# A new plan of a row's stages, with a state ring of twelve steps and three units for x

## The chip, the cores and the metric

The kernel runs on one core of one Trainium2 chip. What counts is the time of one execution on the device in microseconds; the kernel before takes 4036.85 us, the median of three runs. Engines are named as in the profile: PE (TensorE), ACT (ScalarE), DVE (VectorE), POOL (GpSimd), and SP, the engine whose queue issues the DMAs here.

## What is computed

The input is x of 8 images, 48x48 tokens, 256 channels. Cut to what matters, the reference is:

```python
x1 = layernorm(x)                                # over 256 channels
xh, z = split(x1 @ W_in)                         # 512 channels each
xc = depthwise_conv3x3(xh)
dt_r, Bp, Cp = split(xc @ W_xproj)               # 8, 16, 16 columns
dt  = softplus(dt_r @ W_dt + b_dt)
dtN = dt @ W_dtN + b_dtN                         # 16 columns
for t in range(48 * 48):                         # one token of each image a step
    h = exp(dt[t] * A) * h + (dtN[t] * Bp[t]) * xc[t]    # h: 8 images x 512 x 16
    y[t] = h @ Cp[t] + Dskip * xc[t]
x = x + (layernorm(y) * ln_g + ln_b) * silu(z) @ W_out + b_out
t = layernorm(x)
x = x + t + ffn(t)     # ffn: thresholds channels, decodes two nibbles and a shift, and adds 2 at one-hot places
```

## The kernel before, in words

The scan over 2304 steps is the backbone. The states lie on 128 partitions (16 states over two halves of channels, for 8 images); each step has 256 columns for each of two states per partition. DVE updates 192 of the 256 columns, POOL the other 64. For a step DVE does four instructions: `decay_state` multiplies the decay in PSUM (ps_a) with the last state (L869, L872), and `add_input` adds db times x and writes the state (L885, L888). ACT makes the decays by Exp: `decay` (L638) for a pair of steps into one of two ps_a buffers, and `decay_pool` (L648) for POOL's part of four steps, a quad. POOL does one `up` (L1149) for a quad and two instructions for a step (L1159, L1169). PE sums the states of a quad into ps_y (`sum_states`, L492), with the skip term in front of every sixteen steps (`add_skip`, L476); ACT copies ps_y out (`copy_y`). The states stay in a ring of `HRING` steps, and a place is used again once its quad is summed (`c_done`). dt and x reach the scan over DRAM: `store_x` and `store_dt` write a row of 48 steps, `load_x` and `load_dt` spread four steps over the partitions (xb with `XUNITS` units, dtb with three), 512 KB each.

A row has 48 steps, called s. Everything else of the kernel is cut into stages which are hung into these steps, by hand, in the program of each engine. In the row i of the scan PE runs the stages of other rows: LayerNorm transposes and the input projection of row i+4, conv, x_project, dt_project, dtn_project and the transposes for row i+1, z of row i, and the output part of row i-1. `SLOT` gives for each PE stage its steps; the ACT instruction that empties the bank follows in the next step (`s - 1 in SLOT[...]`), and `middle` and `after` say what DVE does between its decay and its add, and behind it. All these PE stages share two PSUM banks in turn: a stage may take its bank when the stage two before it in the order has been emptied (`take_bank`, `emptied_before`). Each engine runs its own list in order, so a wait holds all that stands behind it. ACT's `decay` of a pair waits for the state two pairs back, so ACT can be at most about two steps ahead of DVE.

In the plan before, out_project has the steps 29 to 31 and add_residual 30 to 32; conv 0, 1, 3, 4; the FFN of row i-1 (`ffn_stage`, fourteen stages, two in a step) 40 to 46; gate_y on POOL 21 to 24.

## Time and profile before

| | |
|---|---|
| time, median of three runs | 4036.85 us (4023.55 to 4038.51) |
| the profiled execution, its own time | 4022.24 us |
| its span, first to last instruction | 4020.4 us |
| mean granted TensorE clock | 0.854 |
| PE busy | 3251.8 us, 81% |
| DVE busy | 3622.2 us, 90% |
| ACT busy | 2944.1 us, 73% |
| POOL busy | 3133.2 us, 78% |
| DMA moved | 790.26 MB, mean 197 GB/s |

Busy is the time in which an engine has an instruction in work; a matmul's end is modelled, and neighbouring instructions of one engine overlap a little, so that the distance from start to start is the better price of an instruction than its duration. The granted clock is 1.0 for 2.4 GHz and 0.5 for 1.2 GHz. Times in the rows are microseconds from the span's start unless they are marked ns.

### The profile page before, as it was taken

How to read it: one execution, taken by the hardware profiler on the slowest of the kernel's cores; microseconds unless marked ns; L12 is line 12 of the kernel's file. 1: busy time of each engine (PE TensorE's matmuls, PEld its weight loads, DVE VectorE, ACT ScalarE, POOL GpSimd, SP SyncE). 2: the span in 40 equal slices, each digit the busy share in tenths (PEclk: the TensorE clock that was granted, in tenths of full speed). 3: DMA queues.
4: the chain of work that ended last, by engine and by line, in shares of the span. 5: the costliest groups of instructions: out<-in, count | busy, mean ns of one | idle time of the engine just before them, and what ended most of it. 6: DMA issues, size and time to landing. Idle time of an engine off the chain costs nothing.

```text
span 4020.4 us, 103342 instructions
## 1 busy us (share of the span) xinstructions
PE 3251.8 (81%) x33792; PEld 1589.3 (40%) x33792; DVE 3622.2 (90%) x12317; ACT 2944.1 (73%) x6050; POOL 3133.2 (78%) x5771
## 2 busy tenths in 40 slices
PE   5788888888888888888888888888888888888665
PEld 2334433443344334433443344344433343444333
DVE  2799999999999999999999999999999999999996
ACT  3677777777777787777777777777777777787663
POOL 0788877888888788877888788778877888788874
PEclk7889887889889988988898889888888798889776
DMA  3877878788878787878787878787877888788773
GB/s 67 219 202 203 213 191 206 190 208 205 208 196 214 199 211 196 215 194 205 197 216 199 207 196 213 199 205 193 206 201 199 201 203 209 202 206 205 192 192 80
DMA packets 383392, 790.26 MB, mean 197 GB/s; under 512 B 80517, under 2 KB 235142, under 8 KB 382854
## 3 DMA queue, kind: packets, MB, share of 16 engines
q1 hardware_dynamic: 382854, 783.66, 77.1%
q8 instruction: 268, 4.39, 0.5%
q14 instruction: 270, 2.21, 0.2%
HBM read 648.18 MB, written 96.73 MB: 185 GB/s over the span
## 4 chain that ended last, share of the span: by engine, by line
DVE 31%; PE 31%; ACT 26%; issue 7%; SPq 3%; POOL 2%; DMA 1%; ACTq 0%; POOLq 0%; DVEq 0%
ACT ps_a L638 8%; PE ps_s L583 6%; DVE h L885 6%; PE ps_y L492 6%; PE ps_s L528 4%; DVE ps_a L869 4%; DVE ps_a L872 4%; DVE h L888 4%; PE ps_s L537 3%; ACT ap L648 3%; PE ps_s L566 3%; PE ps_y L476 2%; ACT y L721 2%; DVE sz L941 2%; PE ps_s L584 2%
## 5 line engine op out<-in xcount | busy, mean ns | idle before, releaser
L638 ACT ACTIVATE ps_a<-dtb,a_n 128x384 f32<-128x384 f32 x2304 | 1253.6, 583 | 488.1 <-DVE h L888 472.3
L1169 POOL TENSOR_TENSOR h<-mp,up 128x128 f32<-128x128 f32 x2304 | 1052.5, 457 | 357.6 <-PE ps_y L492 147.4
L1159 POOL TENSOR_TENSOR mp<-ap,h 128x128 f32<-128x128 f32 x2304 | 1051.9, 457 | 358.1 <-ACT ap L648 242.7
L869 DVE TENSOR_TENSOR ps_a<-ps_a,h 128x192 f32<-128x192 f32 x2304 | 813.6, 353 | 239.6 <-ACT ps_a L638 236.7
L885 DVE SCALAR_TENSOR_TENSOR h<-xb,db,ps_a 128x192 f32<-128x192 f32 x2304 | 921.9, 400 | 24.0 <-PE ps_y L492 16.0
L888 DVE SCALAR_TENSOR_TENSOR h<-xb,db,ps_a 128x192 f32<-128x192 f32 x2304 | 927.2, 402 | 0.0
L492 PE MATMUL ps_y<-h,cw 64*32 64x256 f32 x18432 | 787.9, 461 | 71.9 <-DVE h L888 58.0
L872 DVE TENSOR_TENSOR ps_a<-ps_a,h 128x192 f32<-128x192 f32 x2304 | 807.7, 351 | 0.0
L648 ACT ACTIVATE ap<-dtb,a_n 128x256 f32<-128x256 f32 x1152 | 524.2, 509 | 251.1 <-DMA dtb<-xd 233.9
L1149 POOL TENSOR_TENSOR up<-xb,db 128x512 f32<-128x512 f32 x576 | 610.8, 1060 | 3.0 <-DMA xb<-xd 3.0
L492 PEld LDWEIGHTS ps_y<-h,cw 64*32 64x32 f32 x18432 | 315.7, 122 | 488.2 <-DVE h L888 244.6
L511 PE MATMUL ps_s<-xlnT,win 128*128 128x384 f32 x768 | 317.4, 552 | 163.4 <-ACT xh L755 127.1
L528 PE MATMUL ps_s<-xs,conv_w 96*32 96x384 f32 x4608 | 409.9, 506 | 16.7 <-ACT xc L656 8.3
L518 PE MATMUL ps_s<-xlnT,win 128*128 128x384 f32 x768 | 288.2, 509 | 27.1 <-DVE sz L941 26.9
L575 PE MATMUL ps_s<-swap,y 128*128 128x128 f32 x576 | 140.5, 391 | 200.5 <-ACT y L721 173.7
L583 PE MATMUL ps_s<-wout,yn 128*128 128x256 f32 x1152 | 295.8, 401 | 5.5 <-POOL yn L1194 5.5
L551 PE MATMUL ps_s<-xp,wdt 9*128 9x384 f32 x384 | 276.4, 850 | 1.0 <-ACT xp L665 1.0
L511 PEld LDWEIGHTS ps_s<-xlnT,win 128*128 128x128 f32 x768 | 146.6, 206 | 295.2 <-ACT xh L755 154.8
L1189 POOL TENSOR_TENSOR dt<-dt,dttok 128x768 f32<-128x768 f32 x96 | 173.7, 1810 | 108.9 <-ACT dt L698 108.9
L528 PEld LDWEIGHTS ps_s<-xs,conv_w 96*32 96x32 f32 x4608 | 148.4, 114 | 262.1 <-issue 252.0
L583 PEld LDWEIGHTS ps_s<-wout,yn 128*128 128x128 f32 x1152 | 212.4, 194 | 83.0 <-issue 43.1
L476 PE MATMUL ps_y<-skip_w,xc 128*32 128x128 f32 x4608 | 178.6, 303 | 45.6 <-ACT y L762 45.6
(111 smaller groups left out, 4286.5 us busy)
## 6 DMA issues: line engine op xcount, KB each, us to landing
xb<-xd SPq DMA_DIRECT2D x576, 512.0 KB, 7.2
dtb<-xd SPq DMA_DIRECT2D x576, 512.0 KB, 6.3
xs<-xh SPq DMA_DIRECT2D x196, 192.0 KB, 6.2
xd<-dttok SPq DMA_DIRECT2D x288, 128.0 KB, 5.4
xin<-in_x_dram SPq DMA_DIRECT2D x144, 128.0 KB, 6.2
xd<-xtok SPq DMA_DIRECT2D x192, 96.0 KB
res<-in_x_dram SPq DMA_DIRECT2D x144, 128.0 KB, 5.4
out_dram<-res SPq DMA_DIRECT2D x144, 128.0 KB, 3.9
```

The source lines that it names most:

```text
L492: mm = pe.matmul(ps_y[32 * j:32 * j + 32, half, 0:HALF], weights[part, q * P + 32 * j:q * P + 32 * j + 32], h[part, (4 * Q + j) % HRING, n ...
L528: mm = pe.matmul(bank[32 * c:32 * c + 32, 0:TOK], conv_w[0:96, r % 3, dx, NG * c + g, :], xs[0:96, g, c, dx * IMAGES:dx * IMAGES + TOK], s ...
L583: pe.matmul(bank[:, 0:DM], yn[:, g, k * P:(k + 1) * P], wout[:, g, :], start=g == 0, stop=False)
L638: ins = act.activation(ps_a[buf][:, n, 0:2 * VD].rearrange("p (t d) -> p t d", t=2), dtb[:, u % DUNITS, 2 * buf:2 * buf + 2, 0:VD], ACT.Ex ...
L648: ins = act.activation(ap[:, Q % 2, :, n, :], dtb[:, Q % DUNITS, :, VD:HALF], ACT.Exp, scale=a_n[:, n:n + 1])
L869: dve.tensor_tensor(a[:, 0], a[:, 0], last[:, 0], ALU.mult).then_inc(m0_done, 1)
L872: dve.tensor_tensor(a[:, 1], a[:, 1], last[:, 1], ALU.mult).then_inc(m1_done, 1)
L885: dve.scalar_tensor_tensor(h[:, G % HRING, 0, 0:VD], x_t, db[:, r % 2, 0, w:w + 1], a[:, 0], ALU.mult, ALU.add).then_inc(h0_ready, 1)
L888: dve.scalar_tensor_tensor(h[:, G % HRING, 1, 0:VD], x_t, db[:, r % 2, 1, w:w + 1], a[:, 1], ALU.mult, ALU.add).then_inc(h_ready, 1)
L1149: pool.tensor_tensor(up[:, Q % 2], x4, db4.broadcast_to([P, 4, 2, VP]), ALU.mult).then_inc(u_ready, 1)
L1159: pool.tensor_tensor(mp[:, G % 2], ap[:, Q % 2, G % 4], h[:, (G - 1) % HRING, :, VD:HALF], ALU.mult) \
L1169: pool.tensor_tensor(h[:, G % HRING, :, VD:HALF], mp[:, G % 2], up[:, Q % 2, G % 4], ALU.add) \
```

## The change

All stages get new steps. Out_project goes to 23, 24, 25 with add_residual in 24, 25, 26; z to 27 to 30; dtn_project to 31 and the transposes of dt to 32, 33, 35; conv to 40 to 43, for row i+2 now; the projection to 0, 2, 10, 11, for row i+3; x_project to 1; dt_project to 3 and 21, in pairs; the transposes of y to 16 to 19. gate_y moves to POOL's steps 18 to 21, finish_dt to 13 and 26. SP's stores of x and dt are cut into three pieces each, and bounce_states and load_states stand in 34 and 37. The FFN of row i-2 runs in steps 0 to 13, one stage in a step, with twelve stages instead of fourteen: the comparison with 0.5 is folded into the instructions that use it. x_project, dt_project and dtn_project are cut into two halves of the tokens that use different parts of the PE array, and xp and dbt hold 24 positions on twice the partitions. The ring of states has twelve steps, and xb three units.

```diff
-B_ROW, C_ROW, XP_ROWS = 32, 64, 80
+B_ROW, C_ROW, XP_ROWS = 32, 48, 64
-HRING = 8
-XUNITS, DUNITS = 4, 3
+HRING = 12
+XUNITS, DUNITS = 3, 3
 SLOT = {
-    "conv": (0, 1, 3, 4), "xproj": (6,), "dtp": (8, 9, 11, 12), "xtok": (14, 15, 16), "yt": (18, 19, 20, 21),
-    "dttok": (23, 24, 26), "dtn": (27,), "out": (29, 30, 31), "z": (33, 34, 36, 37), "xlnT": (39, 40),
-    "proj": (42, 43, 45, 46),
+    "proj": (0, 2, 10, 11), "xproj": (1,), "dtp": (3, 3, 21, 21), "xtok": (6, 7, 9), "yt": (16, 17, 18, 19),
+    "out": (23, 24, 25), "z": (27, 28, 29, 30), "dtn": (31,), "dttok": (32, 33, 35), "conv": (40, 41, 42, 43),
+    "xlnT": (45, 46),
 }
-AHEAD = {"conv": 1, "xproj": 1, "xtok": 1, "dtp": 1, "dttok": 1, "dtn": 1, "xlnT": 4, "proj": 4, "z": 0, "yt": -1, "out": -1}
+AHEAD = {"conv": 2, "xproj": 1, "xtok": 1, "dtp": 1, "dttok": 1, "dtn": 1, "xlnT": 4, "proj": 3, "z": 0, "yt": -1, "out": -1}
...
# SP
-                    if s == 6 and exists(i - 2):
+                    if s in (8, 10, 12) and exists(i + 1):
+                        store_x(i + 1, (8, 10, 12).index(s))
+                    if s == 13 and 0 <= i + 3 <= SIDE:
+                        load_stack(i + 3)
+                    if s == 14 and exists(i - 2):
                         store(i - 2)
-                    if s == 8 and 0 <= i + 3 <= SIDE:
-                        load_stack(i + 3)
-                    if s == 18 and exists(i - 1):
+                    if s == 19 and exists(i - 1):
                         load_residual(i - 1)
-                    if s == 21 and exists(i + 1):
-                        store_x(i + 1)
-                    if s == 26 and exists(i + 1):
-                        store_dt(i + 1)
-                    if s == 30 and exists(i + 1):
+                    if s == 34 and exists(i + 1):
                         bounce_states(i + 1)
-                    if s == 34 and exists(i + 1):
+                    if s in (35, 36, 38) and exists(i + 1):
+                        store_dt(i + 1, (35, 36, 38).index(s))
+                    if s == 37 and exists(i + 1):
                         load_states(i + 1)
-                    if s == 42 and exists(i + 5):
+                    if s == 47 and exists(i + 5):
                         load_xin(i + 5)
...
# PE: x_project; dtn_project likewise
                 for g in range(NG):
-                    mm = pe.matmul(bank[0:XP_ROWS, 0:TOK], wxp[:, g, :], by_step(xc[:, r % 2, g, :]),
-                                   start=g == 0, stop=g == NG - 1)
+                    for half in range(2):
+                        lo = half * XP_ROWS
+                        mm = pe.matmul(bank[lo:lo + XP_ROWS, 0:HTOK], wxp[:, g, :],
+                                       by_step(xc[:, r % 2, g, :])[:, half * QUADS // 2:(half + 1) * QUADS // 2],
+                                       start=g == 0, stop=g == NG - 1, skip_group_check=True)
...
# DVE, and the same on POOL
-                    if u >= 2:
-                        dve.wait_ge(c_done, u - 1)
+                    if u >= HRING // 4:
+                        dve.wait_ge(c_done, u - HRING // 4 + 1)
...
# DVE: ffn_stage
-                    ins = dve.tensor_scalar(hot[:], hot[:], 0.5, None, ALU.is_gt)
+                    for w in range(3):
+                        ins = dve.scalar_tensor_tensor(score[:, :, w, :], hot[:, :, 32 + 8 * w:48 + 8 * w], 0.5,
+                                                       score16[:].unsqueeze(1).broadcast_to([P, KT, 16]),
+                                                       ALU.is_gt, ALU.mult)
...
# DVE: middle
+                if exists(i - 2):
+                    if s < FFN:
+                        ffn_stage(i - 2, s)
+                    if s == 12:
+                        ffn_mark(i - 2)
+                    if s == 13:
+                        ffn_add_low(i - 2)
                 if exists(i - 1):
                     if s == 6:
                         y_stats(i * KT - 1)
-                    if s == 10:
+                    if s == 11:
                         y_shift_by(i - 1)
-                    if s in (30, 31, 32):
-                        add_residual(i - 1, s - 30)
-                    if s in (33, 34, 35):
-                        ln2_stats(i - 1, s - 33)
-                    if 40 <= s < 47:
-                        ffn_stage(i - 1, 2 * (s - 40))
...
+                    if s in (24, 25, 26):
+                        add_residual(i - 1, s - 24)
+                    if s in (26, 27, 28):
+                        ln2_stats(i - 1, s - 26)
...
# POOL
-                    if s in (16, 17) and exists(i + 1):
-                        finish_dt(i + 1, s - 16)
+                    if s in (13, 26) and exists(i + 1):
+                        finish_dt(i + 1, (13, 26).index(s))
...
-                    if s in (21, 22, 23, 24) and exists(i - 1):
-                        gate_y(i - 1, s - 21)
+                    if s in (18, 19, 20, 21) and exists(i - 1):
+                        gate_y(i - 1, s - 18)
```

## Rows read from the trace of the kernel before

**Rows 1.** Page, part 4: shares of the chain by engine.
```profile
DVE 31%; PE 31%; ACT 26%; issue 7%; SPq 3%; POOL 2%; DMA 1%; ACTq 0%; POOLq 0%; DVEq 0%
```

**Rows 2.** Windows view of the whole scan: length, busy us (instructions), clock, DMA share, GB/s.
```profile
117.00:3982.80 3865.80, 3172.37 (x33438) 1547.63 (x33438) 3587.01 (x12202) 2902.35 (x5966) 3122.69 (x5751) 0.86 0.80 202
```

**Rows 3.** Windows view (PE, PEld, DVE, ACT, POOL) of steps 10-18, 28-32, 40-47 of one row.
```profile
2057.68:2073.98 16.30, 11.26 (x118) 5.50 (x116) 12.41 (x46) 16.30 (x35) 13.86 (x24) 0.63 1.01 223
...
2085.94:2095.38 9.44, 9.44 (x66) 6.08 (x65) 7.68 (x25) 4.58 (x9) 8.49 (x18) 1.00 0.94 253
...
2107.28:2123.91 16.63, 13.27 (x130) 5.62 (x133) 16.63 (x62) 8.03 (x17) 11.96 (x25) 0.90 0.76 196
```

**Rows 4.** Waits view, DVE and ACT: us in total, times, longest us.
```profile
DVE ps_a L869 <- ACT ps_a L638: 236.7, 220, 17.7
...
ACT ap L648 <- DMA dtb<-xd: 233.9, 97, 5.0
```

**Rows 5.** Timeline of DVE, last instruction of two bare steps: start us, us, operation.
```profile
117.34 0.41 DVE L888 SCALAR_TENSOR_TENSOR h<-xb,db,ps_a 128x192 f32<-128x192 f32 x1
...
118.52 0.40 DVE L888 SCALAR_TENSOR_TENSOR h<-xb,db,ps_a 128x192 f32<-128x192 f32 x1
```

**Rows 6.** Lines view, small FFN operations of DVE: count, busy us, mean ns, idle before.
```profile
L978 DVE TENSOR_SCALAR hot<-hot 128x192 f32<-128x192 f32 x48 | 40.5, 843 | 0.0
...
L1027 DVE TENSOR_TENSOR res<-res,hots 128x48 f32<-128x48 f32 x48 | 36.8, 768 | 0.1
L992 DVE TENSOR_TENSOR nib<-best,found 128x9 int32<-128x9 f32 x48 | 33.9, 706 | 0.0
...
L1031 DVE TENSOR_TENSOR res<-res,hots 128x48 f32<-128x48 f32 x48 | 9.5, 198 | 0.1
```

**Rows 7.** Timeline of PE, a state sum and two out blocks.
```profile
2084.48 1.09 PE L492 MATMUL ps_y<-h,cw 64*32 64x256 f32 x32
2085.50 1.99 PE L583 MATMUL ps_s<-wout,yn 128*128 128x256 f32 x8
...
2088.05 1.99 PE L583 MATMUL ps_s<-wout,yn 128*128 128x256 f32 x8
```

**Rows 8.** Around conv: windows of one row, PE's timeline in it and the next.
```profile
1956.54:1962.50 5.96, 5.96 (x60) 2.05 (x64) 5.96 (x27) 3.73 (x8) 3.33 (x8) 0.50 0.67 179
1962.50:1968.50 6.00, 6.00 (x92) 2.11 (x88) 6.00 (x21) 4.25 (x9) 2.75 (x6) 0.98 0.67 171
...
1958.43 8.15 PE L528 MATMUL ps_s<-xs,conv_w 96*32 96x384 f32 x72
...
2115.88 2.46 PE L511 MATMUL ps_s<-xlnT,win 128*128 128x384 f32 x4 [3.36 <-ACT xh L755]
...
2120.01 6.01 PE L528 MATMUL ps_s<-xs,conv_w 96*32 96x384 f32 x72
```

**Rows 9.** POOL: timeline of gate, up and two steps; then finish_dt by line.
```profile
2001.97 1.00 POOL L1194 TENSOR_TENSOR yn<-yn,sz 128x384 f32<-128x384 f32 x1
2002.93 1.06 POOL L1149 TENSOR_TENSOR up<-xb,db 128x512 f32<-128x512 f32 x1
...
2007.02 0.46 POOL L1159 TENSOR_TENSOR mp<-ap,h 128x128 f32<-128x128 f32 x1
...
2008.08 0.46 POOL L1159 TENSOR_TENSOR mp<-ap,h 128x128 f32<-128x128 f32 x1
...
L1189 POOL TENSOR_TENSOR dt<-dt,dttok 128x768 f32<-128x768 f32 x96 | 173.7, 1810 | 108.9 <-ACT dt L698 108.9
```

**Rows 10.** Timeline of ACT, a pair of ps_a and what follows it.
```profile
2079.48 1.13 ACT L638 ACTIVATE ps_a<-dtb,a_n 128x384 f32<-128x384 f32 x2
2080.49 1.11 ACT L677 ACTIVATE dttok<-ps_s 128x512 f32<-128x512 f32 x2
```

**Rows 11.** SP's timeline, twelve x stores; then dtb's issues, KB, us to landing.
```profile
1997.46 8.52 SPq L354 DMA_DIRECT2D xd<-xtok  x12
...
dtb<-xd SPq DMA_DIRECT2D x576, 512.0 KB, 6.3
```

More of the change, by code:

```diff
@@ L148, in build @@
         best = sb("best", [P, KT, 3])
-        found = sb("found", [P, KT, 3])
         nib = sb("nib", [P, KT, 3], I32)
@@ L545, in transpose_xc, with dt_project @@
                 mm.then_inc(xtok_done, 1)
-            def dt_project(r, g):
-                if g == 0:
+            def dt_project(r, pair):
+                if pair == 0:
                     pe.wait_ge(xp_ready, r + 1)
-                bank = take_bank("dtp", r, g)
-                pe.matmul(bank[:, 0:TOK], wdt[:, g * P:(g + 1) * P], xp[0:DTR + 1].rearrange("p b w -> p w b"),
-                          start=True, stop=True).then_inc(dtp_done, 1)
+                banks = [take_bank("dtp", r, 2 * pair + half) for half in range(2)]
+                for n in range(2):
+                    g = 2 * pair + n
+                    for half in range(2):
+                        rows = slice(half * XP_ROWS, half * XP_ROWS + DTR + 1)
+                        mm = pe.matmul(banks[half][:, n * HTOK:(n + 1) * HTOK], wdt[rows, g * P:(g + 1) * P],
+                                       xp[rows].rearrange("p b w -> p w b"), start=n == 0, stop=n == 1,
+                                       skip_group_check=True)
+                        if n == 1:
+                            mm.then_inc(dtp_done, 1)
             def transpose_dt(r, k):
@@ L565, in dtn_project @@
                 for g in range(NG):
-                    mm = pe.matmul(bank[0:B_ROW + NS, 0:TOK], wdtn[:, g, :], dt[:, g, :],
-                                   start=g == 0, stop=g == NG - 1)
+                    for half in range(2):
+                        lo = half * XP_ROWS
+                        mm = pe.matmul(bank[lo:lo + XP_ROWS, 0:HTOK], wdtn[:, g, :],
+                                       dt[:, g, half * HTOK:(half + 1) * HTOK],
+                                       start=g == 0, stop=g == NG - 1, skip_group_check=True)
                 mm.then_inc(dtn_done, 1)
@@ L983, in ffn_stage @@
                     ins = dve.tensor_tensor(amp[:], hot[:, :, 39], hot[:, :, 40], ALU.max)
                 elif n == 3:
-                    dve.scalar_tensor_tensor(amp[:], amp[:], 2.0, hot[:, :, 0], ALU.mult, ALU.mult)
-                    ins = dve.tensor_reduce(best[:], score[:], AX_X, ALU.max)
+                    dve.tensor_scalar(nib[:], best[:], -1.0, 16.0, ALU.mult, ALU.add)
+                    ins = dve.tensor_scalar(amp[:], amp[:], 0.5, 2.0, ALU.is_gt, ALU.mult)
                 elif n == 4:
-                    ins = dve.tensor_scalar(found[:], best[:], 0.0, None, ALU.is_gt)
+                    dve.tensor_single_scalar(nib[:], nib[:], 15, ALU.bitwise_and)
@@ L989, in ffn_stage @@
+                    ins = dve.scalar_tensor_tensor(amp[:], hot[:, :, 0], 0.5, amp[:], ALU.is_gt, ALU.mult)
                 elif n == 5:
[L990 removed]
+                    ins = dve.scalar_tensor_tensor(val[:], nib[:, :, 1], 16.0, nib[:, :, 0], ALU.mult, ALU.add)
                 elif n == 6:
[L992 to L995 removed]
@@ L1134, in _ @@
                     after(i, s)
+            for n in range(FFN):
+                ffn_stage(SIDE - 1, n)
+            ffn_mark(SIDE - 1)
+            ffn_weigh(SIDE - 1)
             ffn_add_low(SIDE - 1)
```

229 lines of the change are left out of this document (110 added, 119 removed).

## The prediction

> **What bounds the kernel now.** I read the windows over the scan first, then the chain, then DVE's waits, and last the timelines of single engines inside one image row. From its first to its last state update the scan takes 3865.8 us, and DVE works in 3587.0 of them [rows 2]. The reader is to see that no other engine comes near: POOL 3122.7, ACT 2902.4. Yet DVE has only 31% of the chain; PE has 31% and ACT 26% [rows 1]. So DVE is the bound on the average and hands over in places. The windows of one row of 79.9 us show where: in its steps 10 to 18 DVE works 12.41 of 16.30 us while ACT is busy in all 16.30, and in steps 28 to 32 it works 7.68 of 9.44; in steps 40 to 47, where the FFN stages lie, it works all the time [rows 3]. DVE's waits say the same: 236.7 us for ACT's ps_a, and ACT in turn 233.9 us for dtb [rows 4].
>
> Per row of 48 steps that is 3865.8 / 48 = 80.5 us, of which DVE works 74.7 and stands 5.8. I call the end of DVE's step s T(s).
>
> **What falls away.** (a) The ACT burst of steps 10 to 18: softplus, xtok, y_norm and scale_yn lie there together. The new plan spreads them from step 4 to 25. I estimate ACT's steps 13 to 22: five pairs of ps_a at 1.01, or 5.1 us [rows 10], and fifteen single ACTIVATEs (ap, y_norm, scale_yn, ln1, parts, copy_y) at about half a pair each, 7.6: 12.7 us, against 13.6 of DVE (ten bare steps of 1.18 [rows 5] and 1.8 for ln1 and the last adds). So this stall goes, 3.9 us in the row shown [rows 3]. (b) The stall of steps 28 to 32, 1.8 us in that row, ends with the late dtb load behind twelve x stores in one piece, 8.5 us on SP [rows 11], which are now three pieces. All 5.8 go, and what is late next is worked out below.
> (c) DVE's own work: is_gt on 192 elements goes, 0.84 us a row, and the chain of found, best, nib with its 0.71 us is two short operations; mark and weigh lose one instruction each; make_db works on half the elements a partition [rows 6]. Against it stand three operations with is_gt folded in, one on amp and one bitwise_and. Means of such small operations hold waits: ffn_add_low and ffn_add_high have the same shape and take 0.77 and 0.20 us [rows 6], and a wait can come back at another instruction. Two instructions fewer at 0.2 give 0.4 us a row as the lower bound, is_gt, nib and three more at 0.2 give 2.2 as the upper; I take 1.2.
> The Trainium skill, "SBUF — State Buffer", section "Who interferes with whom", says that a DVE instruction with two SBUF inputs contends with a GpSimd one that reads SBUF, and that the later one blocks in full. By that rule the 0.71 us of nib are a wait for POOL, which may return wherever POOL is busy, and the saving would be near 0.4, not 1.2; the pair of 0.77 and 0.20 agrees with it.
> (d) x_project, dtn_project and dt_project in two halves save PE time, at most half of their matmuls, and the copy of xp half of ACT's. PE has slack there in the new plan (steps 1, 3 and 21 carry one stage each), so I cost this gain at nothing; if the halves don't overlap, it costs nothing either, as long as PE is idle before step 23.
> (e) The ring of twelve lets DVE and POOL go one quad further before they wait for sum_states. DVE hardly waited for that, and I take zero; without it the conv stage below would cost more. With three x units each load has four steps less: it is issued eight steps, 9.4 us, before its use. I take 0, bounds 0 and 1 us a row.
>
> **What comes: the out-projection.** A bare step takes DVE 1.18 us [rows 5]. From T(19) to the first add_residual, in step 24, DVE has four steps, the aggregates, y_stats and the decay half of step 24: 4.7 + 0.3 + 0.6 + 0.6 = 6.2 us. Without a wait the third, in step 26, stands 9.5 us after T(19). PE can't start out 0 before two things. Its bank is that of the third dtp group, which ACT empties in its step 22; ACT's pair of step 22 waits for T(19), then ln1's logarithm, 1.01 for ps_a and as much for the two parts of the same size [rows 10]: T(19) + 2.7. And it needs all four gates of POOL, now in POOL's steps 18 to 21. POOL's step is 1.06 us (start to start of mp), up adds 1.01, a gate 0.96, a finish_dt 1.8 [rows 9]. From T(12) on: I estimate that POOL starts step 12 about 5 us before T(12), four steps of DVE, since it waits only for ap, which ACT makes in step 11; ten steps from 12 to 21, three up, one finish_dt and four gates are 10.6 + 3.0 + 1.8 + 3.8 = 19.3 us, so the last gate ends at T(12) + 14.4, and T(19) is at T(12) + 9.8. Out 0 starts at T(19) + 4.7.
> Now PE: an out block is 2.55 us and sum_states 1.02 [rows 7], the skip of step 24 about the same. Out 0, skip, sum, out 1, out 2 are 9.7 us: T(19) + 14.4 against 9.5, a stall of 4.9 us at full clock. If POOL were in time it would be 2.7.
> The clock: ahead of the old conv PE stands (3.36 us in one row), and conv's stretch begins at 1.2 GHz: granted clock 0.50 in the 6 us where it starts and 0.98 in the next 6. Three groups took 8.15 us there and 6.01 in the other row, where the level had risen by 2120.0, some 4 us after the gap [rows 8]. In the old steps 10 to 18, light on PE, it is 0.63; in steps 28 to 32, where the old out blocks lie behind dttok and dtn, 1.00 [rows 3]. The new plan puts only transposes, sums and one dtp pair ahead of out, so it starts at the half level. With half speed for 4 to 6 us, as in those two rows, the loss is 2 to 3. The whole stall is then 6.9 to 7.9; I take 7.0, bounds 2.7 and 7.9.
> The Trainium skill, "TensorE: Matmul & The Clock Gate", section "Part 1: The HAM clock gate", says that the throttled state is the default and that activity releases it. By it moving matmuls apart costs speed, which speaks against this plan; with a clock that never fell the stall would be 4.9.
>
> **What comes: conv.** It moves from steps 0 to 4, where DVE had FFN work, to steps 40 to 43, where DVE has bare steps. PE's step 40 begins with add_skip, which waits for copy_y of ACT's step 38, so for T(35) + 1.6. Skip, sum and three conv groups of 2.0 [rows 8] end 8.2 us later at full clock, T(35) + 9.8. ACT copies group 2 in step 43 and makes the ps_a pair 44 behind it, 1.5 us more: T(35) + 11.3. DVE wants it at T(43), eight steps and one y_stats on, T(35) + 10.05. So 1.2 us at full clock, and with 2 to 3 lost at the half level (the same gap lies in front of it) 3.2 to 4.2. I take 3.5, bounds 1.2 and 4.2.
> z and dtn: four z banks pass through DVE's make_sz in steps 29 to 32, right behind the late out blocks, with two table loads on ACT: 0.5 us, bounds 0 and 1.
>
> **The sum.** New stalls 7.0 + 3.5 + 0.5 = 11.0 us a row, old ones 5.8, DVE's work 1.2 less: +4.0 us. Over 47 row periods +190; with head and tail unchanged (117.0 us before the first update, 37.6 behind the last [rows 2]; the same stages in new slots) I add 10 for the FFN stages that now run alone behind the last row. The profiled execution took 4022.2 us, so 4222; the median of the three runs lies 14.6 above it, which gives 4237, and I write **4240**. Its own range is 4130 to 4350.
>
> **The rivals.**
> A, the forecast, 0.55.
> B, DVE alone is the bound, 0.20. The last out block would have to be there by T(19) + 9.5 and conv's third group by T(35) + 8.5: POOL ahead by two more steps, PE at full clock. For it: DVE has the largest sum of work [rows 2]; all other engines have 10 us a row to spare. Against it: the order of the queues, and PE's level in light stretches [rows 3, 8]. Price: stalls of 2.3 instead of 5.8, and 1.2 less work, -4.7 us a row: 4037 - 220 = about 3820.
> C, a chain of transfers at the row's end comes on top, 0.15. dttok is now made in steps 32 to 35. SP queues bounce_states (34), store_dt (35, 36), the loads of step 36, load_states (37, which waits for the bounce) and store_dt (38) before the next row's first load_dt in step 40, and that waits for the last store. By SP's 0.7 us an issue and 6.3 for a transfer to land, the median of dtb, taken for the store too [rows 11], dtb is there at T(35) + 14 to 17; ACT needs it in step 47. Up to about T(35) + 16 conv's stall hides it. The same on the other side: store_x, load_stack and store are 19 transfers in SP's steps 8 to 14, and load_residual of step 19 waits for the store to land. If each bounce takes as long as the old one did under load, 4 us a row come: 4430.
> D, B and A cancel, within 0.5% (about what a measurement of this kernel can tell from no change), 0.05: about 4037.
> E, the halves don't run side by side and PE carries 4 us more of old work, 0.05: out starts no later, since PE stands before it; 4250.
>
> **How the numbers follow.** Slower by over 0.5%: A, C and E, 0.75. Within: 0.05. Faster: 0.20. The range must leave out no more than 2 in 10: most of B lies below 3980 (0.13), and the upper part of C above 4390 (0.06). It is 3980 to 4390.
>
> **What the profile after would show.** Right, if add_residual waits for PE's out block in nearly every row, several us in all; the windows of steps 23 to 26 show a granted clock near 0.5 at first; POOL's last gate ends after T(22); DVE's wait for ps_a lies around steps 42 to 45; ACT is no longer busy without a gap in steps 10 to 18. Wrong, if DVE's busy share rises above 95%; if out blocks end before step 24 begins; if the largest wait of ACT is dtb at the row's end (C); if DVE's work falls by more than 2.2 us a row.

## The result and the profile after

The changed kernel takes 4241.88 us, the median of four runs (4239.21 to 4246.69), beside 4030.2 us for the kernel before on the same chip. The ratio is 1.0526, with an interval of 1.0497 to 1.0555. The prediction said 4240. The profiled execution took 4239.21 us, 217 us more than that of the kernel before.

The rows of after are read in the order of the prediction. First the page's part 4, the chain, which answers to [rows 1]:

```profile
DVE 32%; PE 28%; POOL 16%; ACT 10%; issue 9%; SPq 2%; DMA 2%; POOLq 0%; DVEq 0%; ACTq 0%
```

ACT had 26% and has 10; POOL had 2% and has 16; PE had 31% and has 28. The hand-over has moved from ACT's burst to POOL, and PE keeps its part.

The windows view, with length, busy us of PE, PEld, DVE, ACT, POOL, the clock, the DMA share and GB/s. The first row is the scan [rows 2], with some 7 us ahead of its first state update at 124.05; then come steps 10 to 18 of one row [rows 3], steps 24 to 26, and steps 42 to 47:

```profile
117.00:4200.00 4083.00, 3110.67 (x34542) 1669.14 (x34549) 3535.44 (x12039) 2929.90 (x5969) 3130.79 (x5752) 0.82 0.74 191
2091.49:2105.40 13.91, 6.83 (x110) 3.31 (x109) 13.91 (x47) 12.27 (x24) 12.79 (x22) 0.77 0.81 196
...
2112.43:2125.49 13.06, 13.06 (x93) 7.50 (x92) 5.46 (x18) 6.99 (x12) 11.35 (x21) 0.73 0.87 208
...
2148.31:2159.08 10.77, 10.37 (x154) 4.63 (x146) 7.26 (x25) 8.82 (x19) 7.47 (x15) 1.00 0.68 187
```

In steps 10 to 18 DVE now works all 13.91 us, where it worked 12.41 of 16.30. In steps 24 to 26 it works 5.46 of 13.06 while PE is busy throughout, and in steps 42 to 47 it works 7.26 of 10.77. These are the two stalls that the prediction named.

The waits view of DVE and ACT (total us, times, longest us), which answers to [rows 4]:

```profile
DVE ps_a L891 <- ACT ps_a L655: 328.4, 244, 17.5
DVE res L970 <- PE ps_s L602: 238.3, 110, 11.9
```

```profile
ACT ap L665 <- DMA dtb<-xd: 110.5, 89, 3.4
```

The add_residual of line 970 waits 238.3 us in all for PE's out blocks; in the kernel before the same view has 34.8 us for it. ACT waits for dtb half as long as before.

From the trace of each kernel I also took, for rows 2 to 45, the mean distance from one step's state update to the next and DVE's idle time in it. "Work" is the rest. For one row, in us:

| | row | work | idle | where DVE stands |
|---|---|---|---|---|
| before | 80.71 | 75.16 | 5.56 | steps 10, 16, 18: 3.6; 28, 32: 1.8 |
| after | 85.38 | 74.13 | 11.26 | 24 to 26: 6.46; 32, 34: 1.31; 42, 44: 3.44 |

Of the 6.46 us, 4.8 are waits of the three adds for PE and 1.7 are a wait of DVE's step 24 for ACT's ps_a. PE's timeline around out shows where most of it comes from; each line has start, duration, instruction and, in brackets, the idle time before it with its releaser:

```profile
2106.11 2.20 PE L563 MATMUL ps_s<-xp,wdt 9*128 9x192 f32 x8 [0.23 <-ACT yn L790]
2109.93 3.78 PE L601 MATMUL ps_s<-wout,yn 128*128 128x256 f32 x8 [1.62 <-POOL yn L1212]
2113.64 1.22 PE L602 MATMUL ps_s<-bout,ones_row 1*128 1x256 f32 x2
2114.78 1.94 PE L480 MATMUL ps_y<-skip_w,xc 128*32 128x128 f32 x32
2116.65 1.96 PE L496 MATMUL ps_y<-h,cw 64*32 64x256 f32 x32
2118.54 2.45 PE L601 MATMUL ps_s<-wout,yn 128*128 128x256 f32 x8
2120.92 0.69 PE L602 MATMUL ps_s<-bout,ones_row 1*128 1x256 f32 x2
2121.54 1.99 PE L601 MATMUL ps_s<-wout,yn 128*128 128x256 f32 x8
```

Out block 0 waits for POOL's last gate, then takes 3.78 us where out 2, behind it, takes 1.99 [rows 7]. Skip and sum take 1.94 and 1.96, a sum at the full clock 1.09. So PE starts out at 1.2 GHz and rises near 2119. The windows view has a granted clock of 0.50 for this stretch:

```profile
2109.93:2116.00 6.07, 6.07 (x34) 4.15 (x38) 4.28 (x14) 5.11 (x10) 4.46 (x9) 0.50 1.02 244
```

DVE's timeline has the other side of it:

```profile
2113.53 0.37 DVE L891 TENSOR_TENSOR ps_a<-ps_a,h 128x192 f32<-128x192 f32 x1 [0.99 <-ACT ps_a L655]
...
2114.96 0.42 DVE L970 TENSOR_TENSOR res<-res,ps_s 128x256 f32<-128x256 f32 x1 [0.80 <-PE ps_s L602]
...
2121.65 0.42 DVE L970 TENSOR_TENSOR res<-res,ps_s 128x256 f32<-128x256 f32 x1 [4.87 <-PE ps_s L602]
...
2124.20 0.42 DVE L970 TENSOR_TENSOR res<-res,ps_s 128x256 f32<-128x256 f32 x1 [0.94 <-PE ps_s L602]
```

The second add waits 4.87 us, since skip and sum stand between out 0 and out 1. The wait for ACT in front of the first add lies inside the same delay: the third add can't start before out 2 is done, and that sets the sum of the three stalls. Over rows 2 to 45 the last gate ends at T(19) + 2.90, out 0 starts at T(19) + 2.96, and out 2 is done 12.98 us later: T(19) + 15.9 beside the 9.5 at which the third add stands without a wait.

### The profile page after: what moved, and what is told of

Read it like the earlier page. It is cut to its first block, busy times and chain, and to the rows that moved or that the text cites. A ratio compares the mean times of both kernels' runs of the same rounds, so it can differ in the third digit from the quotient of the medians.

```text
span 4237.4 us, 105655 instructions
## 1 busy us (share of the span) xinstructions
PE 3185.6 (75%) x34944; PEld 1709.0 (40%) x34944; DVE 3571.5 (84%) x12174; ACT 2969.7 (70%) x6050; POOL 3140.5 (74%) x5772
## 4 chain that ended last, share of the span: by engine, by line
DVE 32%; PE 28%; POOL 16%; ACT 10%; issue 9%; SPq 2%; DMA 2%; POOLq 0%; DVEq 0%; ACTq 0%
PE ps_s L601 9%; DVE h L907 6%; PE ps_s L532 6%; DVE ps_a L891 6%; ACT ps_a L655 5%; POOL mp L1177 5%; POOL h L1187 5%; PE ps_y L496 4%; DVE ps_a L894 4%; DVE h L910 4%; POOL yn L1212 3%; PE ps_y L480 3%; PE ps_s L602 3%; POOL dt L1207 2%; DVE res L998 2%
## 5 line engine op out<-in xcount | busy, mean ns | idle before, releaser
L655 ACT ACTIVATE ps_a<-dtb,a_n 128x384 f32<-128x384 f32 x2304 | 1246.6, 575 | 437.9 <-DVE h L910 426.0
L1177 POOL TENSOR_TENSOR mp<-ap,h 128x128 f32<-128x128 f32 x2304 | 1056.2, 458 | 510.6 <-ACT ap L665 396.9
L496 PE MATMUL ps_y<-h,cw 64*32 64x256 f32 x18432 | 775.3, 455 | 95.5 <-DVE h L910 89.1
L1167 POOL TENSOR_TENSOR up<-xb,db 128x512 f32<-128x512 f32 x576 | 611.1, 1061 | 146.3 <-DMA xb<-xd 85.8
L665 ACT ACTIVATE ap<-dtb,a_n 128x256 f32<-128x256 f32 x1152 | 516.9, 498 | 112.9 <-DMA dtb<-xd 110.5
L601 PE MATMUL ps_s<-wout,yn 128*128 128x256 f32 x1152 | 378.3, 484 | 84.5 <-POOL yn L1212 84.5
L480 PE MATMUL ps_y<-skip_w,xc 128*32 128x128 f32 x4608 | 248.7, 385 | 237.8 <-ACT y L781 237.8
L532 PE MATMUL ps_s<-xs,conv_w 96*32 96x384 f32 x4608 | 389.2, 494 | 6.5 <-DMA xs<-xh 6.5
L601 PEld LDWEIGHTS ps_s<-wout,yn 128*128 128x128 f32 x1152 | 264.3, 242 | 211.1 <-POOL yn L1212 122.6
L593 PE MATMUL ps_s<-swap,y 128*128 128x128 f32 x576 | 154.1, 420 | 237.6 <-ACT y L740 122.3
L480 PEld LDWEIGHTS ps_y<-skip_w,xc 128*32 128x32 f32 x4608 | 179.0, 152 | 314.4 <-ACT y L781 280.4
L970 DVE TENSOR_TENSOR res<-res,ps_s 128x256 f32<-128x256 f32 x144 | 60.6, 421 | 246.7 <-PE ps_s L602 238.3
L673 ACT ACTIVATE xc<-ps_s 128x384 f32<-128x384 f32 x192 | 94.2, 490 | 232.5 <-PE ps_s L532 232.5
```

What stands on the lines that cost most here:

```text
L480: mm = pe.matmul(ps_y[32 * j:32 * j + 32, g // 2, g % 2 * P:(g % 2 + 1) * P], xc[:, r % 2, g, lo:lo + 32], skip_w[:, g, :], start=g % 2 == ...
L496: mm = pe.matmul(ps_y[32 * j:32 * j + 32, half, 0:HALF], weights[part, q * P + 32 * j:q * P + 32 * j + 32], h[part, (4 * Q + j) % HRING, n ...
L532: mm = pe.matmul(bank[32 * c:32 * c + 32, 0:TOK], conv_w[0:96, r % 3, dx, NG * c + g, :], xs[0:96, g, c, dx * IMAGES:dx * IMAGES + TOK], s ...
L601: pe.matmul(bank[:, 0:DM], yn[:, g, k * P:(k + 1) * P], wout[:, g, :], start=g == 0, stop=False)
L655: ins = act.activation(ps_a[buf][:, n, 0:2 * VD].rearrange("p (t d) -> p t d", t=2), dtb[:, u % DUNITS, 2 * buf:2 * buf + 2, 0:VD], ACT.Ex ...
L1167: pool.tensor_tensor(up[:, Q % 2], x4, db4.broadcast_to([P, 4, 2, VP]), ALU.mult).then_inc(u_ready, 1)
```

## The experiments

All kernels were timed in turn with the kernel before on the same chip; the ratio is to that one. After has 1.0526. The kernel before differs by up to 0.6% from chip to chip (medians of 4005 to 4030 us), so a difference between two changed kernels is given in us from the ratios, and where the rows of the traces give another figure, that one stands beside it.

### The ring and the x units taken back

```diff
-HRING = 12
-XUNITS, DUNITS = 3, 3
+HRING = 8
+XUNITS, DUNITS = 4, 3
```

> The changed kernel with the state ring of eight steps and four x units, as before: the new plan alone. Theory (the ring buys time only where PE is late, beside out and conv; three x units cost nothing): with eight steps DVE waits in step 44 for the sum of quad 9, which PE makes behind the last conv group, and in step 28 likewise; 1 to 4 us a row more, 4290 to 4430, and waits of DVE's add and POOL's add for ps_y of 50 us or more appear. Rival 1 (the ring does nothing): 4240. Rival 2 (three x units are what makes it slow): below 4200, and POOL's wait of 85.8 us for xb goes.

Measured: 4381.55 us, ratio 1.0923 (1.0875 to 1.0971), as expected. That is some 160 us slower than the changed kernel by the ratios, and 143 by the rows of the traces (88.44 us a row for 85.38). The waits view:

```profile
POOL h L1187 <- PE ps_y L496: 692.8, 308, 5.5
```

In after this wait is 0.8 us. POOL and DVE now stand where a ring place is still to be summed, POOL above all. DVE's idle time is 13.00 us a row for 11.26; its state update of step 24, where it never stood before, has 3.1 of them. Its work is 75.44 for 74.13. I read it so that out and conv keep PE from the sums while eight steps fill up. The prediction took the ring at nothing, because in the old plan DVE hardly waited for it. The two settings were not taken apart here. With four x units POOL's waits for xb, 85.8 us in after, are gone, so the ring alone may be worth more than the two together.

### The FFN stages alone, and with the rings

The twelve new FFN stages in the old plan, in steps 40 to 45; then the same with the ring of twelve and three x units. For room, the FFN's hot and score lie in the dbt tile in the second one, with two more waits on DVE.

```diff
-                    if 40 <= s < 47:
+                    if 40 <= s < 46:
                         ffn_stage(i - 1, 2 * (s - 40))
```

> The kernel before with the new twelve FFN stages alone (steps 40 to 45, mark and weigh in 47), all slots and rings as before. Theory (folded is_gt and shorter nib save DVE 1.0 to 1.2 us a row, all of it on the path since DVE works without a stand in steps 40 to 47): 40 to 60 us faster, ratio 0.985 to 0.990. Rival (the saved instructions held waits that come back elsewhere, or the stalls of steps 10 to 18 grow by as much): 0 to 20 us, ratio 0.995 to 1.000.

> The kernel before with the new FFN stages, and also the ring of twelve and three x units; the slots stay. The FFN's hot and score lie in the dbt tile here, for room. Against the run with the FFN stages alone it is the rings' price in the old plan. Theory of the prediction (DVE hardly waited for the ring, x loads come 8 steps ahead, zero): within 20 us of that run. Rival (the ring lets DVE run on where sum_states is held behind out and conv, as it does by 160 us in the new plan): 40 to 120 us faster than that run. The other rival: three units let the x loads come late around the burst of loads in steps 10 to 18, 20 to 60 us slower.

Measured: 4051.66 us (4024.99 to 4055.40), ratio 1.0094 (1.0057 to 1.0131), for the FFN alone, and 4010.69 us, 1.0007 (0.9990 to 1.0024), with the rings. Both of my expectations failed. The FFN instructions together fall from 10.06 to 9.66 us a row, not by 1.0 to 1.2, and DVE's idle time grows from 5.56 to 6.09. The rings give back 41 us by the medians, where I expected less than 20. The traces have only part of that: the profiled execution of the first kernel took 4024.99 us, 27 us less than its median, so its row of 80.89 us, beside 80.71 before, doesn't show the 0.9%. From 80.89 to the 80.60 of the second kernel, idle grows to 6.36 and work falls from 74.80 to 74.24. What the rings gave in the old plan is therefore not less waiting of DVE.

Why do fewer instructions save so little? Their durations are not their own. In the kernel before, y_shift_by works on three elements a partition. The lines view has it at a mean of 1000 ns, and the new FFN stages alone leave that as it is; with the rings it is 162 ns for the same instruction in the same step of the same plan:

```profile
L934 DVE SCALAR_TENSOR_TENSOR nmy<-mvy,rsy 128x3 f32<-128x3 f32 x48 | 48.0, 1000 | 12.0 <-ACT rsy L732 12.0
```

```profile
L935 DVE SCALAR_TENSOR_TENSOR nmy<-mvy,rsy 128x3 f32<-128x3 f32 x48 | 7.8, 162 | 12.1 <-ACT rsy L731 12.1
```

The timelines of DVE and POOL in the kernel before, at one such place:

```profile
2139.02 1.04 DVE L934 SCALAR_TENSOR_TENSOR nmy<-mvy,rsy 128x3 f32<-128x3 f32 x1 [0.25 <-ACT rsy L732]
```

```profile
2138.98 1.06 POOL L1149 TENSOR_TENSOR up<-xb,db 128x512 f32<-128x512 f32 x1
```

POOL's up runs from 2138.98 to 2140.04, and DVE's instruction ends at 2140.06. In 45 of the 48 rows it starts while up is in work and ends 17 ns behind it, with a spread of 1 ns. So it waits for the end of POOL's instruction, and the trace shows the wait as work. Such a wait goes where POOL's long instructions (up 1.06, gate 1.00, finish_dt 1.82 us) happen to meet such a DVE instruction. The Trainium skill, "SBUF — State Buffer", section "Who interferes with whom", says that a DVE instruction with two inputs from SBUF contends with a GpSimd one that reads SBUF, and that the later one blocks in full; the 17 ns agree. Nor is it only instructions with two inputs: in the kernel before, the is_gt on 128x192, with one, took 1.11 us and ended 116 ns behind up in 29 of 48 rows, and 0.25 us where it met nothing.

### finish_dt later on POOL

```diff
-                    if s in (13, 26) and exists(i + 1):
-                        finish_dt(i + 1, (13, 26).index(s))
+                    if s in (25, 26) and exists(i + 1):
+                        finish_dt(i + 1, (25, 26).index(s))
```

> The changed kernel with one step of POOL moved: the first finish_dt goes from step 13 to step 25, behind the four gates. Theory (out 0 waits for POOL's fourth gate, and PE's gap of 1.62 us in front of it is POOL's lateness): the gates end 1.8 us earlier, out 0 is then bound by its bank, which ACT empties at about T(19) + 2.6, and out 0 starts 0.4 to 1.6 us earlier; 20 to 75 us in all, so 4165 to 4220. PE's wait for POOL yn (84.5 us) falls below 20. Rival (the out blocks' stall is the clock and the order skip, sum, out, not the gates): PE's gap stays for another reason, 4240.

Measured: 4195.4 us, ratio 1.0454 (1.0415 to 1.0494), about 29 us less than after (36 by the rows). The time lies in the expected range, but for another reason. The gates end earlier, at T(19) + 2.47, by 0.4 us and not by 1.8; PE still waits 49.7 us for them, not under 20, and out 0 starts 0.3 us earlier. DVE's idle time hardly changes (11.19 for 11.26 us a row). The gain is in DVE's work, 73.44 for 74.13. The lines view of after, and of this kernel:

```profile
L1034 DVE TENSOR_TENSOR score<-rnib,idx 128x96 f32<-128x96 int32 x48 | 41.4, 863 | 0.0
L1050 DVE TENSOR_TENSOR res<-res,score 128x48 f32<-128x48 f32 x48 | 37.7, 785 | 0.1
```

```profile
L1034 DVE TENSOR_TENSOR score<-rnib,idx 128x96 f32<-128x96 int32 x48 | 21.5, 448 | 0.0
L1050 DVE TENSOR_TENSOR res<-res,score 128x48 f32<-128x48 f32 x48 | 12.7, 264 | 0.1
```

The two instructions lose 0.9 us together, of which the weighing between them takes back 0.2. The timelines of POOL and DVE in after show what held them:

```profile
2094.02 1.82 POOL L1207 TENSOR_TENSOR dt<-dt,dttok 128x768 f32<-128x768 f32 x1
2097.84 1.06 POOL L1167 TENSOR_TENSOR up<-xb,db 128x512 f32<-128x512 f32 x1
```

```profile
2095.19 0.77 DVE L1034 TENSOR_TENSOR score<-rnib,idx 128x96 f32<-128x96 int32 x1
2098.14 0.83 DVE L1050 TENSOR_TENSOR res<-res,score 128x48 f32<-128x48 f32 x1
```

The first ends 0.11 us behind finish_dt, in 45 of 48 rows, and the second 0.06 us behind the up that finish_dt had pushed back, also in 45. The experiment meant for the gates showed the block of DVE by POOL.

### The FFN under conv

The twelve FFN stages go from steps 0 to 11 to steps 36 to 47 of the row before, and what follows them (mark, weigh and the two adds) from steps 12 and 13 to 0 and 1.

```diff
+                if exists(i - 1) and s >= 36:
+                    ffn_stage(i - 1, s - 36)
...
```

> The changed kernel with DVE's FFN work moved from steps 0 to 13 to steps 36 to 47 of the row before and steps 0 and 1, so that it lies beside conv, as in the kernel before. Theory (conv's 3.4 us of DVE idle in steps 42 and 44 come from conv lying beside bare DVE steps): these 3.4 us and the 0.45 of step 34 go, PE, ACT and POOL have enough room in steps 0 to 13 (ACT has about 17 us of work there, DVE then 18), 3.4 to 3.9 us a row, 4060 to 4085. Rival (the sum of the slack is what counts, and the stall moves into steps 0 to 22): within 4200 to 4250.

Measured: 4203.11 us, ratio 1.0465 (1.0427 to 1.0504). The stalls of steps 42 and 44 are gone (3.44 us a row), and the stall of step 24 grows from 2.04 to 4.55. Steps 0 to 13 are now shorter than POOL's and ACT's work in them, so the gates come later: out 0 starts at T(19) + 5.4, and PE waits 166.0 us for the gates, after 84.5. The slack moved, as the rival said: idle is 11.05 us a row for 11.26. The 24 us gained (39 by the rows) are mostly in DVE's work, 73.49 for 74.13.

### PE filled in steps 13 to 19

```diff
+                    if exists(i) and s in FILL:
+                        fill(FILL[s])
```

Here `FILL = {13: 6, 14: 6, 16: 4, 17: 4, 18: 4, 19: 4}` and the matmuls write unused columns of ps_y, which spoils part of y's sums; so my expectation that they change no output was wrong.

> The changed kernel with 28 extra 128x128x128 matmuls a row on PE in its steps 13 to 19, where PE stands idle; they write columns of ps_y that nobody reads, so they change no output. Theory (out starts at 1.2 GHz because PE has little to do in steps 13 to 22, and that costs about 4.5 us of the stall): the granted clock in the out blocks rises to near 1.0 and the time falls by 2 to 4 us a row, 4050 to 4150. Rival (the stall is the order and the gates, the clock follows from it): the clock rises, the time stays within 4220 to 4250. If the extra matmuls come in the way of the transposes of y, the gates come later and the time rises.

Measured: 4242.2 us, ratio 1.0568 (1.0531 to 1.0605). It didn't test what it was made for. The windows and timeline of PE:

```profile
2112.00:2116.00 4.00, 3.44 (x49) 2.33 (x49) 4.00 (x18) 2.68 (x7) 3.75 (x7) 1.00 1.00 235
2116.00:2120.00 4.00, 2.27 (x7) 1.18 (x4) 4.00 (x15) 2.59 (x7) 3.76 (x7) 0.66 0.95 235
```

```profile
2114.78 2.10 PE L564 MATMUL ps_s<-xp,wdt 9*128 9x192 f32 x8 [0.56 <-ACT yn L797]
2118.61 3.78 PE L602 MATMUL ps_s<-wout,yn 128*128 128x256 f32 x8 [1.73 <-POOL yn L1219]
```

The clock was at 2.4 GHz until the dt_project pair was done, and fell at 2117.30, in the gap of 1.73 us behind it. Out 0 took 3.78 us as before. The pair itself, whose matmuls use nine rows of the array, took 2.10 us here at a granted clock of 1.00 and 2.20 in after at 0.50. I took from this that the fill has to stand directly ahead of out.

### dt_project early, without and with a fill ahead of out

```diff
-"dtp": (3, 3, 21, 21)
+"dtp": (3, 3, 5, 5)
...
+                    for _ in range(16):
+                        pe.matmul(bank[:, 0:P], ident[:], ident[:], start=True, stop=True, skip_group_check=True)
                     pe.wait_ge(gated, r * NG + NG)
```

The slot is in both kernels, the fill (and 8 such matmuls ahead of yt 0) in the second alone.

> The changed kernel with one slot moved: the second dt_project pair goes from PE's step 21 to step 5 (its softplus parts on ACT from steps 22 and 23 to 6 and 7). It takes the 9-row matmuls (2.20 us at the half clock) from the place just ahead of out block 0, and out 0's bank then waits for nothing that is late. My theory of the out stall: POOL's fourth gate and the half clock set it, so little comes of this, 4200 to 4250 where the changed kernel takes 4240, ratio 1.043 to 1.055 to the kernel before; PE's gap ahead of out 0 grows from 1.6 to about 3.8 us. Rival (the bank that ACT's step 22 frees sets it): out 0 starts 1 to 2 us earlier and the time falls by 45 to 90 us, to 1.03 to 1.04.

> As the run with dt_project early, and PE works 8 small matmuls into yt block 0's own bank while it waits for y_norm, and 16 into out block 0's own bank while it waits for the gates; the outputs are the same. It tells what the clock costs at the out blocks. Theory (the half clock is worth 3 to 4.5 us a row there): out 0 takes 2.0 to 2.5 instead of 3.8 us, skip and sum 1.1 instead of 1.95 each, out 0 to out 2 span 10 to 11 instead of 14 us, DVE's stall in steps 24 to 26 falls from 6.5 to 2 to 3.5 us, the time by 130 to 210 us against the kernel without the fill, ratio 1.00 to 1.02. Rival (the out stall is POOL's, the clock only moves the wait): out 0 is faster but the three adds of DVE wait as before for a POOL step or an ACT step, less than 40 us.

Measured: 4353.53 us, ratio 1.0859 (1.0831 to 1.0886), without the fill, and 4242.35 us, 1.0583 (1.0562 to 1.0603), with it. PE's timeline with the fill:

```profile
2114.35 4.94 PE L602 MATMUL ps_s<-ident 128*128 128x128 f32 x32
2120.56 1.99 PE L605 MATMUL ps_s<-wout,yn 128*128 128x256 f32 x8 [1.28 <-POOL yn L1216]
2122.49 0.69 PE L606 MATMUL ps_s<-bout,ones_row 1*128 1x256 f32 x2
2123.11 1.08 PE L480 MATMUL ps_y<-skip_w,xc 128*32 128x128 f32 x32
2124.12 1.09 PE L496 MATMUL ps_y<-h,cw 64*32 64x256 f32 x32
```

Out 0 to out 2 fall from 12.64 to 9.75 us, the mean over rows 2 to 45; the prediction had 9.7 for the full clock. DVE's stalls of steps 24 to 26 fall by the same 2.9 us a row, from 7.5 to 4.6. Of these 2.1 reach the row, since the stalls of steps 12 and 42 grow by 1.0, and 111 us the whole. The size expected for the block was right; the stall left (2 to 3.5) and the gain of the whole (130 to 210 us) were not, and the ratio of 1.0583 is far from the 1.00 to 1.02 expected.

The first of the two kernels fits neither of its expectations, 1.043 to 1.055 and 1.03 to 1.04. By the ratios it is 130 us slower than after, by the rows of the traces 95 (87.42 for 85.38 us). I put that down to softplus's four instructions (1.9 us), which now stand in ACT's steps 6 and 7, where ACT has ap to make for POOL:

```profile
POOL mp L1177 <- ACT ap L665: 577.7, 229, 8.6
```

In after this wait is 396.9 us. DVE has a new stall of 0.9 us in step 12, and the gates end at T(19) + 4.24 instead of 2.90. The bank of out 0 was free, and it brought nothing: the gates set the start.

### A plan mended by these findings

Four kernels, each built on the one before it. First: dt_project's second pair in step 14, where ACT has little to do in step 15; the two fills; finish_dt late; the adds one step later.

```diff
-"dtp": (3, 3, 21, 21)
+"dtp": (3, 3, 14, 14)
...
-                    if s in (24, 25, 26):
-                        add_residual(i - 1, s - 24)
+                    if s in (25, 26, 27):
+                        add_residual(i - 1, s - 25)
```

> The changed kernel with the causes of the out stall that the runs so far showed, each treated: the second dt_project pair in PE's step 14 (its softplus parts in ACT's 15 and 16, where ACT has least to do), 8 small matmuls into yt 0's bank and 16 into out 0's bank while PE waits, both finish_dt in POOL's 25 and 26, and the three add_residual in steps 25 to 27 instead of 24 to 26 (statistics one step later too). Theory (clock 2.4 us a row, POOL's finish_dt some 1.5, one step 1.2): out 0 starts at T(19) + 2.5 to 3, the stalls around out fall from 6.5 to 1.5 to 2.5 us, the row to 80.5 to 81.5 us, the time to 0.995 to 1.015 of the kernel before. Rival 1 (the dt pair costs ACT in step 15 and 16 what it cost in 6 and 7, through ap and POOL): 1.02 to 1.04. Rival 2 (a later add holds the banks of z): stalls in steps 29 to 32 grow from 1.3 to over 2.5 us.

Measured: 4098.63 us, ratio 1.0182 (1.0165 to 1.0199), just above the expected range. Idle falls to 9.04 us a row. The stalls around out are 2.7, but those of conv grow from 3.4 to 4.2, out 0 starts at T(19) + 3.7 and not + 2.5 to 3, and step 18 has a new stall of 0.4: the fill ahead of yt ran at half clock, 3.78 us, into the work behind it.

Second: 22 small matmuls into conv 0's bank ahead of the skip of step 40.

> As the run before it, and PE works 22 small matmuls into conv 0's own bank ahead of the skip of step 40, while it waits for copy_y (3.8 us before). Theory (skip and sum ran at half clock, 1.8 and 1.96 us where the full clock gives 1.1 each): conv's first group starts 1.7 us earlier and the stalls of steps 42 and 44 fall from 3.4 to 1.7 to 2 us, 70 to 80 us less, ratio 0.975 to 0.995. Rival (the stall is ACT's copies or the transfer of dtb behind it): under 25 us less.

Measured: 4104.99 us, ratio 1.0195 (1.0178 to 1.0211): no gain, where 0.975 to 0.995 was expected. Skip and sum do take 1.08 and 1.09 us, and the stall of step 42 falls by 1.0. But the fill took 5.18 us where the gap was 3.82, so the skip starts 1.2 us later, and DVE's work grows by 0.7 us a row, all of it in the FFN instructions; I take it that they meet POOL's otherwise. The first kernel's SP queue and ACT show what else was late:

```profile
2115.53 3.02 SPq L356 DMA_DIRECT2D xd<-xtok  x4
2118.65 3.31 SPq L345 DMA_DIRECT2D xs<-xh  x4
2122.01 2.69 SPq L424 DMA_DIRECT2D out_dram<-res  x3
2124.80 0.57 SPq L390 DMA_DIRECT2D dtb<-xd  x1
```

```profile
2130.62 0.91 ACT L669 ACTIVATE ap<-dtb,a_n 128x256 f32<-128x256 f32 x2 [2.86 <-DMA dtb<-xd]
```

Eleven transfers in a row hold the dtb load of step 16 on SP, and ACT's step 23 waits 2.86 us for it.

Third: load_stack behind those loads, and smaller fills (4 ahead of yt, 15 ahead of the skip).

```diff
-                    if s == 13 and 0 <= i + 3 <= SIDE:
+                    if s == 25 and 0 <= i + 3 <= SIDE:
                         load_stack(i + 3)
```

> As the mended kernel with conv filled, and load_stack (four transfers) goes from SP's step 13 to step 25, behind the dtb loads of steps 16 and 20; the fills are smaller (4 matmuls ahead of yt, 15 ahead of the skip of step 40), since they ran into the work behind them. In the mended kernel SP needs 17 us from its first x store to the dtb load of step 16, and ACT's ap of step 23 waits 2.9 us for that load in the row looked at. Theory (SP's queue now sets the stall of steps 18 to 24): this stall, 1.7 us a row, falls to 0.5 or less, 50 to 80 us less, ratio 1.000 to 1.010. Rival (ACT's own work and the late pair 24 set it): under 20 us.

Measured: 4039.41 us, ratio 1.0038 (1.0020 to 1.0056), as expected. ACT's waits for dtb fall from 172.7 to 107.2 us, the stalls of steps 18 and 24 (0.7 and 1.1 us a row) are gone, and idle is 7.03 us a row. Step 42 also falls, from 1.7 to 0.5, where the skip again starts at T(35) + 2.4 behind the smaller fill. On the other side step 26 waits 0.8 more, and step 0 has a new stall of 0.8. How much of the whole is the queue and how much the smaller fills was not taken apart.

Fourth: the first four FFN stages, the two large ones among them, in steps 40 to 43.

```diff
+                if exists(i - 1) and 40 <= s < 44:
+                    ffn_stage(i - 1, s - 40)
                 if exists(i - 2):
-                    if s < FFN:
-                        ffn_stage(i - 2, s)
+                    if s < FFN - 4:
+                        ffn_stage(i - 2, s + 4)
```

> As the run before it, and the first four FFN stages of a row (some 5 us of DVE work, the two large ones among them) go from steps 0 to 3 of the next row to steps 40 to 43, where DVE waits for conv. Theory (work laid into the stall of 3.2 us there): the stalls of steps 42 and 44 fall to under 0.5, 2.5 us a row or 120 us less, ratio 0.970 to 0.985. Rival (as when the whole FFN went there: steps 0 to 3 then have less work for DVE than ACT and POOL need, and the time comes back as stalls in steps 10 to 24): 0 to 50 us less, ratio 0.99 to 1.01.

Measured: 3916.03 us (3909.07 to 3920.42), ratio 0.9729 (0.9707 to 0.9750). This is less than both kernels: 2.7% less than before. Its page:

```profile
PE 3298.8 (84%) x38244; PEld 1950.7 (50%) x38244; DVE 3513.1 (90%) x12174; ACT 2942.0 (75%) x6050; POOL 3133.4 (80%) x5772
```

The stalls of steps 42 and 44 (1.9 us) and that of step 0 are gone; idle is 5.43 us a row, work 72.88. The out stall grew by less than one us (3.1 for 2.5), where the move of the whole FFN had cost 2.5. The rest of the gain, 1.3 us of work a row, is again the small instructions; that was luck, not plan, and the time lies in the expected range only with it. Set beside the kernel before, this holds for nearly all of the 2.7%: DVE's idle time is 5.43 us a row for 5.56, its work 72.88 for 75.16. The last plan stands as long as the old one did and works less, partly through the new FFN stages and partly through shorter waits for POOL; the two parts were not measured apart.

## Why the prediction was right, by its own steps

**(a), (b) The old stalls.** Right: DVE stands nowhere in steps 10 to 18 nor 28, and 5.6 us a row are gone. A late dtb still plays a part elsewhere: in the row shown ACT waits 0.94 us for it just before the ps_a that DVE's step 24 waits for.

**(c) DVE's work.** The sum was close, -1.0 us a row for -1.2, and the step was wrong. The FFN instructions became dearer in their new place, 10.67 us a row after 10.06, although there are three fewer; alone in the old place they save 0.4. What fell is y_shift_by (1000 to 154 ns), ln1_shift_by (806 to 257) and make_db (610 to 406), 1.6 us a row, and of these only make_db was in the reckoning. The means of small instructions were read as their prices, and they are in part waits for POOL. The estimate by the rule, 0.4, was the better one for the fold.

**(d)** Right: PE's work for x_project and dtn_project falls to 55% (134.8 to 73.0 us and 133.1 to 74.3), that for dt_project to 75% (276.4 to 206.2), and PE stands ahead of out.

**(e) The ring.** Wrong. Its price was read from the waits of the old plan. In the new plan ring and x units together are worth some 140 to 160 us. The forecast didn't need the price, since both kernels that it compares have the ring that goes with their plan, but its remark that conv would cost more without the ring names the smaller place: most of DVE's stands at the ring are in step 24, beside out.

**Out-projection.** 6.5 us against 7.0, with terms that miss in both directions. POOL's last gate ends at T(19) + 2.9, not + 4.7, and so before T(22), which is at T(19) + 3.7; the sign that I had named for it failed. POOL does start its step 12 5.2 us before T(12), but with the up of that quad already made, which my sum counts again (1.0 us), and DVE needs 10.4 us from T(12) to T(19), not 9.8. From out 0 to out 2 it takes 13.0 us, not 11.7 to 12.7. The half clock costs 2.9 of that by the two kernels that differ in the fills alone, which is within my 2 to 3, and 3.2 from after to the filled one. The two misses, 1.8 us too late and 0.3 to 1.3 us too short, take back part of each other; that the stall came so near to 7.0 is in part luck. (The lower bound of 2.7 is a slip: out 0 at T(19) + 2.7 and 9.7 behind it give 2.9 by my own terms.)

**Conv.** 3.4 us against 3.5, again with two misses in opposite directions. The skip of step 40 starts at T(35) + 2.4, not 1.6. Behind it the half clock costs 1.6 us, not 2 to 3, and in most rows only in skip and sum; conv itself then runs at the full clock, four groups in 7.95 us. With the clock mended by the smaller fill 1.9 us are left, where I had 1.2. PE's timeline:

```profile
2143.18 1.80 PE L480 MATMUL ps_y<-skip_w,xc 128*32 128x128 f32 x32 [3.82 <-ACT y L781]
2144.91 1.96 PE L496 MATMUL ps_y<-h,cw 64*32 64x256 f32 x32
```

**z and dtn.** 1.3 us, above the bound of 1: steps 32 and 34 wait 0.86 and 0.45 us a row, the same in every kernel of the new plan but the one with the old rings. What sets them was not looked into.

**The sum.** Stalls +5.7 instead of +5.2 and work -1.0 instead of -1.2 make +4.7 us a row in rows 2 to 45, where I had 4.0. The profiled executions differ by 217 us: the scan takes 4075.5 us for 3865.8, 210 more where I had 190, the head 7.0 more (the first state update is at 124.05, not 117.01), the tail 0.3. My 10 us stood for the FFN stages behind the last row, and they didn't come, while the head, which I had left unchanged, took 7.0. On the 4222 of the sum I put 14.6 us for the distance from the profiled execution to the median, and in after that is 2.7. So 17 us too few, 12 too many and 3 of rounding make the 4240 agree with 4241.88 to 2 us. That nearness is luck; the mechanism and the size of the two large stalls are not.

**The rivals.** B put DVE alone as the bound at 3820, with two conditions: POOL ahead and PE at full clock. The last kernel nearly meets the second (its mean granted clock is 0.93, after's 0.82) and works around the first, and takes 3916. Yet it doesn't show B's mechanism: DVE still stands 5.4 us a row, not 2.3, and what made it fast is less work. C's sign, dtb as ACT's largest wait, does not show: dtb has 110.5 us, DVE's state 426.0. C's chain at the row's end is not seen. Its other side probably is: with the transfers of steps 8 to 14 thinned out on SP the stall of step 24 went, though the fills were changed in the same kernel. E did not occur: by the figures under (d) the three halved stages take 4.0 us a row less of PE.

Open is how to get POOL's gates earlier: in the last kernel they still end at T(19) + 4.0, and step 26 waits 2.1 us. POOL starts its step 12 there 2.4 us before T(12), in the third kernel of that plan 4.9. I read it so that DVE, with less FFN work in its steps 0 to 13, leaves POOL less of a lead.

## What to carry to other kernels

A stage that moves carries along what stood in front of it: here dense matmuls moved behind light PE work started at half clock, and small matmuls into the waiting stage's own bank gave that back, at a loss where they ran past the gap. Where the mean of a small DVE instruction is far above that of its like, lay the timelines of DVE and POOL side by side before the mean is taken for a price; here it was a wait for POOL. And a buffer that hardly anybody waits for in one plan may carry the next.

## What the runs showed of the hardware

A DVE instruction on three elements a partition took 1.04 us beside POOL's up and ended 17 ns behind it, in 45 of 48 rows with a spread of 1 ns. Moving one POOL instruction of 1.8 us changed two DVE instructions from 863 and 785 to 448 and 264 ns.

In the kernel with PE filled in steps 13 to 19, the granted clock stayed at 1.00 through eight matmuls over nine rows of the array (2.10 us) and fell to 0.50 in the gap of 1.73 us behind them. Such a group took 2.10 us at 1.00 and 2.20 at 0.50, while out 0 took 1.99 and 3.78. The Trainium skill, "TensorE: Matmul & The Clock Gate", section "Part 1: The HAM clock gate", says that the throttled state is the default and activity releases it; the fills agree with that, and no run here separates the part of the gap from that of the nine rows.
